# The q/k/v stage of a macaron transformer block: all short convolutions on VectorE, gate groups spread between the units, new orders on all engines

## What is computed

```python
x = layernorm(x)                                   # over 512 features
def short_conv(x, w):                              # w: [512, 4], causal over time
    return sum(shift(x, 3 - i) * w[:, i] for i in range(4))
q = silu(short_conv(x @ Wq + bq, q_conv))          # 16 heads of 32
q = q / (norm(q) + 1e-6)
k = silu(short_conv(x @ Wk + bk, k_conv)); k = k / (norm(k) + 1e-6)
v = silu(short_conv(x @ Wv + bv, v_conv))
alpha, beta = sigmoid(x @ Wa + ba), sigmoid(x @ Wb + bb)
out_gate = silu(x @ Wg + bg)
```

## Time and profile before

| | us |
|---|---|
| median of 3 runs | 3521.77 (3519.32 to 3527.73) |
| the profiled execution, its own time | 3522.09 |
| its span from first to last instruction | 3520.3 |
| q/k/v stage, first memset to the first issue of the next phase | about 608.8 to 1624.8 |

### The profile page before, as it was taken

How to read it: one execution, slowest core, us unless ns; L and a number is a source line. 1 busy time by engine, 2 the same in 40 slices (tenths; PEclk the granted TensorE clock), 3 DMA queues, 4 the chain that set the end, 5 groups by cost and what they waited for, 6 DMA issues and landing times. The chain is left out here.

```text
span 3520.3 us, 192119 instructions
## 1 busy us (share of the span) xinstructions
PE 3247.0 (92%) x83236; PEld 2732.5 (78%) x83236; DVE 2775.2 (79%) x4456; ACT 1567.9 (45%) x2328; POOL 1832.7 (52%) x1707
## 2 busy tenths in 40 slices
PE   7999998698989999894999999999996987999999
PEld 5888886476666667673999999999995765888887
DVE  6767765788888888874899999999997866676765
ACT  4555453577777777772121211121213433545454
POOL 1232322466666666654778888778884431222232
PEclk8999999799999999997999999999997998999999
DMA  3122222232323223224677777777774772212121
GB/s 120 71 101 78 91 88 86 84 91 90 92 86 98 88 79 107 74 86 126 185 201 202 198 200 201 199 199 198 201 199 138 235 226 111 100 71 107 71 107 60
DMA packets 486556, 452.96 MB, mean 129 GB/s; under 512 B 55504, under 2 KB 448848, under 8 KB 467280
## 3 DMA queue, kind: packets, MB, share of 16 engines
q1 hardware_dynamic: 484176, 449.56, 42.4%
q10 hardware_dynamic: 2304, 2.49, 0.3%
HBM read 331.33 MB, written 120.60 MB: 128 GB/s over the span
## 5 line engine op out<-in xcount | busy, mean ns | idle before, releaser
L350 POOL TENSOR_TENSOR ffn_out<-ffn_gate,ffn_xres 128x512 f32<-128x512 f32 x128 | 179.9, 1437 | 781.5 <-DVE ffn_gate L254 781.1
L803 DVE SCALAR_TENSOR_TENSOR ain_conv<-ain_padded,ain_taps,ain_conv 128x512 f32<-128x512 f32 x384 | 447.7, 1166 | 13.6
L1480 ACT ACTIVATE rec_u<-rec_ps_end 128x256 f32<-128x256 f32 x128 | 49.0, 383 | 632.4 <-PE rec_ps_end L1532 632.4
L902 POOL TENSOR_TENSOR ain_conv<-ain_conv,ain_term 128x512 f32<-128x512 f32 x192 | 281.3, 1465 | 16.0
L1248 POOL TENSOR_TENSOR rec_d_norm<-rec_dmat,rec_early 128x512 f32<-128x512 f32 x128 | 162.7, 1271 | 174.7 <-DVE rec_dmat L1330 174.7
L957 ACT ACTIVATE ain_buf<-ain_conv 128x512 f32<-128x512 f32 x192 | 120.9, 630 | 244.5 <-POOL ain_conv L902 158.8
L46 PE MATMUL ffn_ring<-ffn_mixkh,ffn_wkh 128*128 128x512 f32 x512 | 218.8, 427 | 6.5 <-DVE ffn_mixkl L196 6.5
L46 PE MATMUL ffn_ring<-ffn_mixrh,ffn_wrh 128*128 128x512 f32 x512 | 215.6, 421 | 9.2 <-DVE ffn_mixrl L306 9.2
L899 POOL TENSOR_SCALAR ain_term<-ain_padded,ain_taps 128x512 f32<-128x512 f32 x192 | 185.9, 968 | 39.7 <-POOL ain_conv L902 26.4
L46 PE MATMUL ffn_ring<-ffn_mixkh,ffn_wkl 128*128 128x512 f32 x512 | 203.3, 397 | 0.0
L46 PE MATMUL ffn_ring<-ffn_mixrh,ffn_wrl 128*128 128x512 f32 x512 | 202.3, 395 | 0.0
(11 more groups left out here) (252 smaller groups left out, 10218.7 us busy)
## 6 DMA issues: line engine op xcount, KB each, us to landing
rec_early<-coeffs SPq DMA_DIRECT2D x512, 128.0 KB, 3.0
streams<-ain_buf SPq DMA_DIRECT2D x48, 1024.0 KB, 5.1
rec_qkv<-streams SPq DMA_DIRECT2D x126, 384.0 KB, 3.3
rec_qk_pe<-streams SPq DMA_DIRECT2D x127, 256.0 KB, 3.3
rec_late<-coeffs SPq DMA_DIRECT2D x504, 64.0 KB, 2.3
ffn_xres<-in_x SPq DMA_DIRECT2D x16, 1024.0 KB
ain_x<-x SPq DMA_DIRECT2D x16, 1024.0 KB, 4.8
gate<-ain_gate SPq DMA_DIRECT2D x16, 1024.0 KB, 6.6
```

Source lines behind the costliest of these rows:

```text
L350: added = nc.gpsimd.tensor_tensor(out[:, m, :], gate[:, m, :], xres[:, m, :], ALU.add)
L803: nc.vector.scalar_tensor_tensor(out=out[:], in0=pad[:, n:n + TOK], scalar=taps[:, u // KT, u % KT, n:n + 1], in1=out[:], op0=ALU.mult, op ...
L902: nc.gpsimd.tensor_tensor(out[:], out[:], term[:], ALU.add).then_inc(pool_conv, 1)
L1480: nc.scalar.activation(u[:], ps_end[:, :, 1, :], ACT.Copy).then_inc(u_ready, 1)
```

## The change

All of it is in `attn_in_phase`.

- VectorE convolves all 12 units; GpSimd keeps only `squares`. `term` goes, and `gamma_norm` has a buffer of its own instead of that of `alpha_beta`.
- TensorE: q, k and v go round three PSUM buffers and the gate has the fourth; a gate group stands behind every three units. `mean` is done two tiles ahead, behind the second gate group.
- ScalarE, VectorE: written-out orders; `centre` and the square two tiles ahead, `norms` and its root one tile late, `decays` last; `variances` is split from `deviations`.
- SyncE: decay rows behind the v store and before the gate's store; the rows of the norms of tile t-1 between the q and the k store of tile t, x three tiles ahead. The last tile's inverse norms are issued by ScalarE.

The core of the diff:

```diff
 @block.sync
-            def slot(pair, s, ahead):
+            def slot(pair, s, ahead=True, first=False):
                 t = pair * 4 + s
-                if ahead:
-                    load_x(t + 2)
-                for j in range(3):
-                    sp.wait_ge(silued, 12 * t + 4 * j + 4)
-                    store_stream(t, j)
-                    if j == 1:
-                        sp.wait_ge(ends_ready, t + 1)
-                        store_rows(pair, s, K_DECAY, decay, Q_ROWS)
-                        for m in range(KT):
-                            sp.dma_start(last_decay[:, m, bass.ds(t * CPT, CPT)], gamma_end[m * HD:m * HD + HG, :]).then_inc(coeff_stored, 16)
+                sp.wait_ge(silued, UNITS * t + 4)
+                store_stream(t, NQ)
+                if not first:
+                    store_norms(pair - (s == 0), (s - 1) % 4)
+                sp.wait_ge(silued, UNITS * t + 8)
+                store_stream(t, NK_)
+                if ahead:
+                    load_x(t + 3)
+                sp.wait_ge(silued, UNITS * t + 12)
+                store_stream(t, NV)
+                sp.wait_ge(ends_ready, t + 1)
+                store_rows(sp, pair, s, K_DECAY, decay, Q_ROWS, decay_stored)
                 for m in range(KT):
+                    sp.dma_start(last_decay[:, m, bass.ds(t * CPT, CPT)], gamma_end[m * HD:m * HD + HG, :]).then_inc(decay_stored, 16)
                 sp.wait_ge(gate_ready, KT * t + 2 * KT)
                 sp.dma_start(gate_dram[bass.ds(t, 1), :, :, :].rearrange("a p k n -> (a p) k n"), gate[:]).then_inc(gate_stored, 16)
-                sp.wait_ge(norm_ready, t + 1)
-                store_rows(pair, s, K_QNORM, inv_norm, Q_ROWS)
...
 @block.vector
-            def slot(t, s, ahead):
+            def slot(t, s, ahead=2, first=False):
                 mask_tails(t)
+                for u in range(3):
+                    convolve(t, u)
                 if ahead:
-                    centre(t + 1)
-                for u in (0, 1, 3, 4):
-                    convolve(t, u)
-                decays(t)
+                    variances(t + 1)
                 if ahead == 2:
                     sums(t + 2)
-                convolve(t, 6)
+                convolve(t, 3)
                 if ahead:
                     deviations(t + 1)
+                convolve(t, 4)
+                convolve(t, 5)
+                if not first:
+                    norms(t - 1)
+                if ahead:
+                    normalise(t + 1)
+                convolve(t, 6)
                 convolve(t, 7)
                 if ahead:
-                    normalise(t + 1)
-                convolve(t, 9)
+                    low(t + 1, 1 - s)
+                convolve(t, 8)
+                if ahead == 2:
+                    centre(t + 2)
+                if not ahead:
+                    decays(t)
+                for u in range(9, UNITS):
+                    convolve(t, u)
                 if ahead:
-                    low(t + 1, 1 - s)
-                convolve(t, 10)
-                norms(t)
+                    decays(t)
 @block.gpsimd
-            with pool.Fori(0, NT - 1) as t:
-                slot(t, True)
-            slot(NT - 1, False)
+            squares(1)
+            with pool.Fori(2, NT) as t:
+                squares(t)
 @block.scalar
+            def gates(t, m):
+                if m == 0:
+                    act.wait_ge(gate_stored, 16 * t)
+                    act.wait_ge(w_split["g"], 1)
+                act.wait_ge(group_done, 16 * t + 4 * m + 4)
+                nc.scalar.activation(gate[:, m, :], ring[3][:], ACT.Silu, bias=bias[:, 3, m:m + 1]).then_inc(gate_ready, 1)
+            def slot(t, s, ahead=2, first=False):
+                for u in range(3):
                     shift(t, u)
+                silu(t, 0, ahead)
+                gates(t, 0)
+                shift(t, 3)
+                silu(t, 1, ahead)
+                silu(t, 2, ahead)
+                shift(t, 4)
+                if ahead:
+                    deviation(t + 1)
+                decay_rates(t)
+                shift(t, 5)
+                if not first:
+                    head_norms(t - 1)
+                silu(t, 3, ahead)
+                silu(t, 4, ahead)
+                gates(t, 1)
+                shift(t, 6)
+                shift(t, 7)
+                silu(t, 5, ahead)
+                if ahead:
+                    high(t + 1, 1 - s)
+                shift(t, 8)
+                gates(t, 2)
+                silu(t, 6, ahead)
+                silu(t, 7, ahead)
+                shift(t, 9)
+                silu(t, 8, ahead)
+                shift(t, 10)
+                if ahead == 2:
+                    act.wait_ge(heads_summed, HEADS_0 + 2 * t + 1)
+                    square(t + 2)
+                silu(t, 9, ahead)
+                shift(t, 11)
+                if not ahead:
+                    head_norms(t)
+                silu(t, 10, ahead)
+                silu(t, 11, ahead)
+                gates(t, 3)
 @block.tensor
+            def gate_product(t, s, m):
+                pe.wait_ge(gate_ready, KT * t + m + KT)
+                product(nc, ring[3][:], *W["g"], m, xh[s], xl[s]).then_inc(group_done, 1)
...
+                for u in range(UNITS):
...
+                    pe.wait_ge(biased, BIASED_0 + UNITS * t + u - 2)
+                    product(nc, ring[u % 3][:], *W["qkv"[j]], m, xh[s], xl[s]).then_inc(group_done, 1)
+                    if u == 2:
+                        pe.wait_ge(w_split["g"], 1)
+                        gate_product(t, s, 0)
+                    if ahead and u == 3:
+                        var(t + 1)
                     if u == 5:
+                        gate_product(t, s, 1)
+                        if ahead:
+                            spread_rstd(t + 1)
+                        if ahead == 2:
+                            mean(t + 2)
+                    if u == 8:
                         pe.wait_ge(heads_selected, 1)
+                        head_sums(t, 0)
+                        gate_product(t, s, 2)
+                if not ahead:
+                    head_sums(t, 1)
+                gate_product(t, s, 3)
+                if ahead:
+                    head_sums(t, 1)
```

More of the change, by code:

```diff
@@ L638, in _ @@
                     sp.dma_start(ab_bias[at:at + HG, :], ab_bias_dram[head:head + HG, :]).then_inc(ab_loaded, 16)
-            for n in "kvg":
+            for n in "gkv":
                 sp.dma_start(stage[n], w_dram[n]).then_inc(w_loaded[n], 16)
@@ L679, in slot @@
-                store_rows(pair, s, K_BETA, gamma_norm, B_ROWS)
             load_x(1)
-            with sp.Fori(0, PAIRS - 1) as pair:
+            load_x(2)
+            for s in range(4):
+                slot(0, s, first=(s == 0))
+            with sp.Fori(1, PAIRS - 1) as pair:
                 for s in range(4):
-                    slot(pair, s, True)
+                    slot(pair, s)
             for s in range(4):
-                slot(PAIRS - 1, s, s < 2)
+                slot(PAIRS - 1, s, ahead=(s < 1))
@@ L763, in centre @@
             def centre(t):
+                if not isinstance(t, int) or t > 0:
+                    dve.wait_ge(x_low, t)
                 dve.wait_ge(mean_done, t + 1)
@@ L766, in centre, with variances, deviations @@
                                         ALU.subtract).then_inc(centred, 1)
-            def deviations(t):
+            def variances(t):
                 dve.wait_ge(var_done, t + 1)
                 nc.vector.tensor_scalar_add(var_tok[:], ps_mean[:, 0:KT], LN_EPS).then_inc(var_copied, 1)
+            def deviations(t):
                 dve.wait_ge(std_ready, t + 1)
@@ L852, in _ @@
             select_heads()
+            place_ab()
             dve.wait_ge(ident_step, 2)
+            variances(0)
             deviations(0)
@@ L856, in _ @@
             normalise(0)
-            place_ab()
+            sums(1)
             low(0, 0)
-            sums(1)
             bias_taps()
+            centre(1)
             choose_rows()
[L862 to L866, removed]
+            slot(0, 0, first=True)
+            with dve.Fori(0, NT // 2 - 2) as r:
+                slot(2 * r + 1, 1)
+                slot(2 * r + 2, 0)
+            slot(NT - 3, 1)
+            slot(NT - 2, 0, ahead=1)
+            slot(NT - 1, 1, ahead=0)
+            norms(NT - 1)
         @block.gpsimd
@@ L880, in squares @@
                 nc.gpsimd.tensor_tensor(sum2, half2[:, 0, :], half2[:, 1, :], ALU.add).then_inc(summed2, 1)
[L882 to L909, removed]
             squares(0)
+            weight_low("g")
             weight_low("v")
-            weight_low("g")
-            with pool.Fori(0, NT - 1) as t:
-                slot(t, True)
-            slot(NT - 1, False)
+            squares(1)
+            with pool.Fori(2, NT) as t:
+                squares(t)
         @block.scalar
@@ L1000, in _ @@
             act.sem_inc(heads_summed, HEADS_0)
```

(34 more changed lines are left out.)

125 lines of the change are left out of this document (50 added, 75 removed).

## The result

The changed kernel takes **3438.7 us** (median of 4 runs, 3437.6 to 3448.8) against 3520.6 us (4 runs, 3516.0 to 3527.7) before: ratio 0.977, 95% interval 0.9749 to 0.9792. The prediction was 3448, range 3400 to 3488.

The account below looks back on a forecast made before the run. GpSimd's convolutions were taken to hold back ScalarE, it VectorE, and it TensorE, at 60.28 us a tile. Gains of 51 us (13 tiles), 8.5 and 14.2 (edges) make 74, from 3522.1 to 3448 us; range 3400 to 3488.

Parts of the forecast that it names:

- TensorE's own 52.7: TensorE's work alone per tile: 47.6 us of matmuls plus 2.4 and 2.7 of small products, 52.7 us.
- VectorE's work: VectorE's steps per tile with GpSimd quiet, all 12 units included: 48.9 us, less than today's 51.3.
- Rival D: VectorE's multiply-adds stay at 1.18 us though GpSimd is quiet: 3752 us; decided from a mean of 0.91 us; chance 0.05.
- The value near the dear end: GpSimd's `squares` beside units 9 to 11 cost VectorE 3.4 us a tile, upper end 3.7.
- the lower end of the term: `squares` cost VectorE nothing if its back-to-back stream keeps GpSimd out.
- The new wait: ScalarE's early gate SiLU waits for the previous tile's gate store; VectorE then waits 1.6 us before unit 3.
- D + 10.0: Gate store's landing, counted from D, the end of `decays` on VectorE; range D + 8 to D + 12.7.
- the walk: Step-by-step count of one tile from the end of `decays`: 10.0 + 46.35 = 56.35 us a tile, today 60.28.
- TensorE's wait for the diagonal: Wait before `spread_rstd` stays at its old size, costing nothing since TensorE has 3.6 us to spare.
- The sum: Gain of 51 us over 13 tiles, 8.5 at tile 0 and 14.2 in the last two tiles: 74 us.
- then without waits: VectorE from `deviations` through units 4 to 11 to `decays` never waits, ScalarE being ready 1 us or more earlier.
- Rival B: TensorE becomes the bound: store lands before ScalarE wants it, GpSimd doesn't hold VectorE; period 53, 3404 us; chance 0.17.

Follow-up runs that it names:

- e1: Kernel before with only the convolutions moved (VectorE convolves all 12 units, old orders kept): 3421.5 us, ratio 0.971.
- e6: Changed kernel with the two additions of `squares` done by VectorE behind unit 9 instead of GpSimd: 3431.5 us, ratio 0.9743.
- e5: Changed kernel with the gate's store ahead of the decay rows and VectorE's loop written out: 3401.6 us, ratio 0.9658.
- e9: e3 with 24 one-column memsets in front of VectorE's loop, loop kept: 3403.2 us, ratio 0.9659.
- e3: Changed kernel with the gate's store issued right behind the v store, ahead of the decay rows: 3432.6 us, ratio 0.9744.
- e4: Changed kernel with VectorE's loop written out so that it never jumps: 3430.7 us, ratio 0.9738.
- e8: e1 with 60 one-column memsets in front of VectorE's loop: 3424.7 us, ratio 0.9724.
- e10: e1 with 40 memsets in front of VectorE's loop: 3417.5 us, ratio 0.9703.

## Why the prediction was right, and what it missed

**The bound of before** was read rightly: ScalarE's waits for GpSimd, handed on to VectorE's root and TensorE's diagonal, and GpSimd's additions blocking VectorE (a multiply-add at 1166 ns before, 776 in e1). e1 takes just these two away, together, and gains 102 us. Of the 7.6 us between the old period and TensorE's own 52.7, the wait for the diagonal is 3.9 (51.0 in 13 tiles). Behind the one of the earlier trace rows TensorE is slower for a while: from 1173.5 to 1176.0 the granted clock is 0.50, and the two steps from 1175.84 to 1176.69 take 0.43 us each instead of 0.234.

**VectorE's work**: 48.9 us without GpSimd plus 3.4 for `squares`. Measured: units step at 2.65 us, the blocked copy and multiply-adds cost 2.20 + 0.91 = 3.1 us. Rival D (0.91 us a multiply-add) is out at 0.776. The value near the dear end was right, and e6 confirms the sign. GpSimd's two additions beside the copy and the multiply-adds of unit 10:

```profile
1138.51 2.87 POOL L909 TENSOR_TENSOR ain_half<-ain_sq 128x1024 f32<-128x1024 f32 x1 [51.99 <-ACT ain_sq L925]
1141.45 1.30 POOL L911 TENSOR_TENSOR ain_half<-ain_half 128x512 f32<-128x512 f32 x1
```

```profile
1141.64 1.67 DVE L819 SCALAR_TENSOR_TENSOR ain_conv<-ain_padded,ain_taps,ain_conv 128x512 f32<-128x512 f32 x1
```

The multiply-add began 0.19 us behind the second addition and ended 0.56 us after it, 1.67 us instead of 0.75, so it stood for 0.9 us of the 1.1 that were left. The copy began 0.53 us behind the first addition and ended with it, at 1141.40, 2.36 us instead of 0.16. Both times it was VectorE that stood. What decides which of the two engines stands, no run shows; the lower end of the term, nothing, was my estimate.

**The new wait**: in the tile shown the gate's store landed at D + 10.1 (predicted D + 10.0), unit 3 began at D + 12.0 (D + 12), and the period without the jump is 56.2 (56.35). That close a match holds for this tile alone. The store's issue came at D + 4.2 to D + 5.2 (I took 4.9) and the landing 4.0 to 4.8 us behind it (5.1), so the first tiles of the pairs take 55.0 us on average without the jump, and the walk was 1.3 us a tile too dear there. From the landing on the walk was right within 0.3 us: in each of the seven tiles of the 13 in which ScalarE stands 3.8 us or more, the period without the jump is the landing plus 46.1 us (46.35). TensorE's wait for the diagonal was to stay; it is 24.4 us in 9 tiles of the stretch 700 to 1430.

**The sum**: 13 tiles 51 us predicted, 783.7 - 725.1 = 58.6 measured; tile 0 and what is before it 8.5 predicted against 10.8, of which 1.5 is that the phase began that much sooner; the last two tiles 14.2 against 13.8. Total 74 predicted against 83 measured, the difference of the two profiled executions being 3522.1 - 3438.4 = 83.7.

**The step that failed** is "then without waits", from unit 9 through `decays` into the next tile. The walk had no term for the loop's jump. It costs 4.8 us every second tile, and it did not show in the time because the tile behind it skips the gate's wait and the root's wait, and is 4.4 us shorter than the walk: 61.03 + 51.92 = 112.95 against 2 x 56.35 = 112.7. So the agreement of the period is in this part luck, two errors that cancel: a stall left out, and in the pairs a wait counted twice as often as it acts. The 7.5 us by which the 13 tiles came out cheaper (58.6 against 51) are mostly the store's earlier landing: the other pairs take 111.1 to 112.0 us, the three tiles outside the pairs 56.1, 55.6 and 54.2.

**Rival B** had the right price: 3404 for "the gate's store is not waited for, TensorE is the bound" is what e5 and e9 measure, 3401.6 and 3403.2. Its conditions were not the right ones. It needed the stall gone, which it did not name. The store need not land before ScalarE wants it: in e5 ScalarE waits up to 2.6 us for it. And GpSimd may hold VectorE: e5 has `squares` on GpSimd and TensorE at 100%.

**What the prediction did not ask** is what each part of the change is worth. It credited the orders with removing the start's wait (3.2 us a tile, true) and charged them with the gate's wait, but did not sum the two: by e1 the balance was 17 us to the bad. The walk of the old orders without GpSimd's units would have given it, had it let ScalarE's inherited waits go as well.

## What to carry to other kernels

Walk a large change also with only its strongest part in place; here one engine's move is worth 102 us and the reorderings around it minus 17, until one store is issued a few lines earlier and the stall at the jump is gone too; then the new orders are some 20 us better than the old. Where a single buffer's store is queued behind small transfers that wait for the last work of a tile, put the large store first. And when two repairs give little alone, try them together before dropping either: 6 and 8 us became 37.

## What the runs showed of the hardware that I had not expected

VectorE stood 4.8 to 6.6 us at the jump back of a loop of some 285 instructions (my count in the listing), and the profile names it only as "issue". The same loop moved 24 instructions further on (e9 against e3) stands 0.4 to 0.5 us, with 16 packets on the instruction queue in the stretch 720 to 1400 where there were 40. The changed kernel has 40 of them there too, three in the 8 us from 1152, at the jump of 1155; e1 has 17, none in the 12 us from 1084, at its jump of 1088; e4, without a jump, has 20. So the stall and the packets come and go together. That VectorE stands for a fetch of instructions is my reading of this; no trace shows it. At which code positions it stands, e8 and e10 do not let me say.

The gate's store of 1 MB landed 4.2 us (changed kernel) and 3.9 us (e4) after its issue, median, when issued some 7 us behind the v store, and 7.1 us (e3, e5) after it when issued 0.6 to 0.7 us behind the v store; before, 1.2 us behind, it was 6.6. Issuing it sooner was still right: in e3 it goes out at D - 1.6 to D - 1.4 instead of D + 4.2 to D + 5.2 and has landed at D + 5.5 to D + 5.7 instead of D + 8.2 to D + 10.1, in the tiles without a stall in front.
